# A gated recurrence and a routed expert layer on one core: another order in the sequences, list scatters spread out, another opening

## The reference

```python
def reference(x, ...):                      # x: 8 sequences x 512 tokens x 256, float32
    xn = layernorm(x)
    # recurrence
    g, v, d = xn @ Wg + bg, xn @ Wv + bv, xn @ Wd + bd        # 256 x 256 each
    h = linear_scan(sigmoid(g) * tanh(v), a=0.001 + 0.998 * sigmoid(d))   # along the 512 tokens
    # 8 experts, the best two of each token, and one shared expert
    scores = sigmoid(xn @ gate.T + b + bias)
    top2 -> weights[token, expert]
    y = sum_e weights[:, e] * (gelu(xn @ W1[e].T + b1[e]) @ W2[e].T + b2[e])   # 256 -> 1024 -> 256
    shared = gelu(xn @ Ws1.T + bs1) @ Ws2.T + bs2
    return x + h + y + shared
```

## Time and profile before

| | before |
|---|---|
| median of 3 runs | 729.48 us (728.88 to 731.09) |
| profiled execution | 729.41 us, of which span 727.1 us |
| mean granted TensorE clock | 0.986 |
| busy: TensorE, VectorE, ScalarE, GpSimd | 91%, 72%, 59%, 42% of the span |
| phase 1, opening included | 0 to about 315 us |
| phase 2 | about 315 to 727 us |

### The profile page before, as it was taken

How to read it: one execution, slowest core, us unless ns; L and a number is a source line. 1 busy time by engine, 2 the same in 40 slices (tenths; PEclk the granted TensorE clock), 3 DMA queues, 4 the chain that set the end, 5 groups by cost and what they waited for, 6 DMA issues and landing times.

```text
span 727.1 us, 20160 instructions
## 1 busy us (share of the span) xinstructions
PE 664.5 (91%) x5816; PEld 516.4 (71%) x5817; DVE 523.6 (72%) x1381; ACT 431.7 (59%) x738; POOL 303.5 (42%) x261
## 2 busy tenths in 40 slices
PE   2679898999898999779999999999999999999993
PEld 1246565556555565568888888888888888888773
DVE  4579897979888898866666676666676666666652
ACT  6766767686767766445555555555555555554651
POOL 2015252524343343414464464464464554453521
PEclk9899999999999999999999999999999999999998
DMA  8407170716162624112332332332332332332421
GB/s 266 150 2 188 44 174 32 175 29 173 30 173 36 167 51 123 46 44 50 60 65 53 63 65 52 63 62 54 64 63 53 65 58 58 65 59 52 74 39 22
DMA packets 54172, 57.55 MB, mean 79 GB/s; under 512 B 13204, under 2 KB 48916, under 8 KB 54136
## 3 DMA queue, kind: packets, MB, share of 16 engines
q1 hardware_dynamic: 38456, 38.42, 19.7%
q0 software_dynamic: 15680, 18.69, 16.1%
HBM read 38.53 MB, written 18.55 MB: 79 GB/s over the span
## 4 chain that ended last, share of the span: by engine, by line
PE 60%; DVE 21%; issue 8%; ACT 7%; DMA 1%; DVEq 1%; POOL 0%; ACTq 0%; SPq 0%; POOLq 0%
PE bank L1150 26%; PE bank L1142 24%; DVE W L767 4%; DVE arena L863 3%; PE bank L1169 3%; DVE arena L864 2%; PE bank L1199 2%; ACT W L605 2%; PE bank L1181 2%; ACT arena L569 2%; PE bank L1130 2%; DVE arena L806 1%; DVE small L776 1%; ACT arena L562 1%; DVE arena L795 1%
## 5 line engine op out<-in xcount | busy, mean ns | idle before, releaser
L1150 PE MATMUL bank<-W,arena 128*128 (+1 forms) x2304 | 304.6, 274 | 22.3 <-DVE arena L864 21.7
L1142 PE MATMUL bank<-rows,W 128*128 128x256 f16 (+1 forms) x1920 | 301.3, 295 | 4.6 <-issue 3.3
L1150 PEld LDWEIGHTS bank<-W,arena 128*128 128x128 f16 x2304 | 221.3, 98 | 66.6 <-DVE arena L864 31.7
L1142 PEld LDWEIGHTS bank<-rows,W 128*128 (+1 forms) x1920 | 186.7, 99 | 59.2 <-issue 3.8
L576 ACT ACTIVATE arena<-bank,par 128x256 f32<-128x256 f32 x256 | 133.8, 559 | 83.7 <-PE bank L1142 73.1
L490 POOL DMA_INDIRECT out<-arena,slot_add x64 | 109.5, 1710 | 149.9 <-ACT arena L688 140.2
L863 DVE TENSOR_SCALAR arena<-arena,par 128x256 f16<-128x256 f32 x284 | 101.7, 358 | 83.4 <-ACT arena L576 53.6
L864 DVE SCALAR_TENSOR_TENSOR arena<-arena,par 128x256 f16<-128x256 f32 x284 | 138.8, 489 | 10.1
L432 POOL DMA_INDIRECT lists<-entry,place x64 | 83.5, 1305 | 118.2 <-DVE entry L860 101.1
L475 POOL DMA_INDIRECT rows<-xhl_rows,slot_list x64 | 68.9, 1077 | 46.0 <-DMA slot_list<-lists 22.9
L1130 PE MATMUL bank<-rows,W 128*128 128x512 f16 x288 | 67.1, 392 | 6.2 <-ACT arena L562 6.2
(11 more groups left out here) (158 smaller groups left out, 542.4 us busy)
## 6 DMA issues: line engine op xcount, KB each, us to landing
stage<-in_w SPq DMA_DIRECT2D x32, 512.0 KB, 6.2
b2row<-in_b SPq DMA_DIRECT2D x39, 128.0 KB
arena<-in_x SPq DMA_DIRECT2D x8, 512.0 KB
xhl_rows<-W SPq DMA_DIRECT2D x8, 512.0 KB
out<-arena SPq DMA_DIRECT2D x8, 512.0 KB
W<-in_w SPq DMA_DIRECT2D x4, 512.0 KB, 8.4
lists<-entry,place POOLq DMA_INDIRECT x64
rows<-xhl_rows,slot_list POOLq DMA_INDIRECT x64
```

The costliest lines, as they stand in the source:

```text
L1142: ins = T.matmul(bank_, weights(w, wp * HALF + c * H + j * P, P), rhs[:, 2 * xp + c, :], start=n == 0, stop=n == 3 * KD - 1)
L1150: ins = T.matmul(banks[t // 2][:, (t % 2) * D:(t % 2 + 1) * D], h[:, hp, t * P:(t + 1) * P], weights(w, (2 + wp) * HALF + j * D, D), start ...
```

## The change

`sequence` gets a new order on four engines. In ScalarE's, `squares` of the next set move: one each behind projections 1 and 4 and behind GELUs 0 and 1 (before: behind projections 1, 3, 4 and 5); `normed` and `x_high` move one GELU later, and `score` moves up behind projection 4. In VectorE's, `scan_input(b, ch)` waits for one event less, `places` moves up to stand behind split 0, the `residual`s move from splits 3 and 4 to 2 and 3, the first `low_part` moves from split 5 to 4, and the second stands behind `add_bias`. `scales` shrinks from 13 instructions to 8 (the power of two is taken from the exponent of the sum directly). On TensorE `ranks` moves one projection up, `norm_sum` becomes two accumulating matmuls into bank `ps_l` and also waits for `place_ok`, and the `scan_transposes` and `x_transposes` move one block up each. In the last sequence `places` moves ahead of `shared_result`, the three `tables` parts move from splits 0, 1, 2 to 1, 2, 4, and set 8's preparation moves up.

The eight `scatter`s of a sequence, until now issued back to back, are spread: the first waits for `place_ok`, the others for the event numbers in `SPREAD`, counted from the sequence's start; numbers over 14 lie in the next sequence.

The opening has functions of its own. The two halves of x's transposes go to two banks; 24 and 12 dummy matmuls (`WARM`) are put around them; routing, layer by layer splitting and the recurrence are interleaved. The constant list contents are built in another part of the arena.

```diff
+SMALLEST = float(48 << 23)
+WARM = 24
+SPREAD = {None: (10, 11, 13, 14, 16, 18, 20), SEQS - 2: (9, 10, 11, 12, 13, 14, 15), SEQS - 1: (4, 5, 6, 7, 8, 9, 10)}
-        spare = arena[:, 6144:6656].bitcast(U32)
-        zeros = arena[:, 6656:7168]
+        spare = arena[:, 0:512].bitcast(U32)
+        zeros = arena[:, 512:1024]
+        ps_low16 = ps_e[3][:, :].bitcast(F16)
@@ gpsimd
-            def scatter(b):
+            def scatter(b, c):
                 u = b % 2
-                pool.wait_ge(entry_ok, 2 * b + 2)
-                pool.wait_ge(place_ok, b + 1)
-                for c in range(2 * TPB):
-                    pool.indirect_dma_start(...)
+                if c == 0:
+                    pool.wait_ge(entry_ok, 2 * b + 2)
+                    pool.wait_ge(place_ok, b + 1)
+                else:
+                    pool.wait_ge(ev_act, RING + b * EVENTS + SPREAD.get(b, SPREAD[None])[c - 1])
+                pool.indirect_dma_start(...)
             for b in range(SEQS):
+                for c in range(4, 7):
+                    if b:
+                        scatter(b - 1, c)
                 if b + 1 < SEQS:
                     rstd(b + 1)
-                scatter(b)
+                if b:
+                    scatter(b - 1, 7)
                 if b + 1 < SEQS:
                     fill_entries(b + 1)
+                for c in range(4 if b + 1 < SEQS else 8):
+                    scatter(b, c)
@@ scalar
+            def opening():
+                for i in range(2):
+                    projection(0, 0, i)
+                for part in range(2):
+                    high_part(0, 0, part)
+                projection(0, 0, 2)
+                decay(0, 0)
+                projection(0, 0, 3)
+                projection(0, 0, 4)
+                high_part(0, 1, 0)
+                projection(0, 0, 5)
+                high_part(0, 1, 1)
+                act.wait_ge(spare_out, 64)
+                gelu_wide(0, 0, 0)
+                decay(0, 1)
+                score(0)
+                squares(1, 0, 0)
+                gelu_wide(0, 0, 1)
+                squares(1, 0, 1)
+                gelu_wide(0, 0, 2)
+                normed(1, 1)
+                gelu_wide(0, 0, 3)
+                squares(1, 1, 0)
+                gelu_wide(0, 0, 4)
+                squares(1, 1, 1)
+                act.wait_ge(xhl_out, 16)
+                x_high(1)
+                ...
             def sequence(b, u, last_=False):
                 for i in range(PROJ):
                     projection(b, u, i)
                     if i in (2, 5):
                         decay(b, i // 3)
-                    if not last_:
-                        if i == 1:
-                            squares(b + 1, 0, 0)
-                        if i >= 3:
-                            squares(b + 1, (i - 2) // 2, (i - 2) % 2)
+                    if i == 1:
+                        squares(b + 1, 0, 0)
+                    if i == 4:
+                        score(b)
+                        squares(b + 1, 0, 1)
                 for i in range(KH):
                     gelu_wide(b, u, i)
-                    if i == 0:
+                    if i in ((1, 2) if last_ else (0, 1)):
+                        squares(b + 1, 1, i - last_)
+                    if i == 1 and not last_:
                         normed(b + 1, 1 - u)
-                    if i == 1:
+                    if i == 2 and not last_:
                         act.wait_ge(xhl_out, b * 16 + 16)
                         x_high(b + 1)
-                    if 3 <= i < 7:
-                        high_part(b + 1, (i - 3) // 2, (i - 3) % 2)
+                    k = i - 4 if last_ else i - 3
+                    if 0 <= k < 4:
+                        high_part(b + 1, k // 2, k % 2)
@@ vector
+            def opening():
+                for part in range(5):
+                    best_two(0, part)
+                scales(0)
+                variances(1, 1)
+                for part in range(2):
+                    low_part(0, 0, part)
+                scan_input(0, 0)
+                scan(0, 0)
+                for part in range(2):
+                    low_part(0, 1, part)
+                scan_input(0, 1)
+                split_wide(0, 0)
+                scan(0, 1)
+                split_wide(0, 1)
+                places(0, 0)
+                split_wide(0, 2)
+                dve.wait_ge(bs2_in, 16)
+                add_bias(0, 0)
+                own.settle()
+                residual(0, 0, 0)
+                split_wide(0, 3)
+                residual(0, 0, 1)
+                split_wide(0, 4)
+                scales(1)
+                x_low(1)
+                split_wide(0, 5)
+                low_part(1, 0, 0)
+                split_wide(0, 6)
+                low_part(1, 0, 1)
+                split_wide(0, 7)
+                add_bias(1, 1)
             def sequence(b, u, last_=False):
                 if last_:
                     for part in range(5):
                         best_two(b, part)
+                for part in range(2):
+                    low_part(b, 1, part)
+                if last_:
+                    places(b, u)
+                shared_result(b - 1, 0)
+                shared_result(b - 1, 1)
                 ...
                 for i in range(KH):
                     split_wide(b, i)
                     if i == 0:
+                        if not last_:
+                            places(b, u)
                         scan(b, 1)
+                    if i == 1 and not last_:
+                        scales(b + 1)
+                    if i == 3 and last_:
+                        scales(b + 1)
                     if i == 2:
-                        places(b, u)
-                        x_low(b + 1)
+                        if not last_:
+                            x_low(b + 1)
+                        dve.wait_ge(o_out, b * 16)
+                    if i in (2, 3):
+                        residual(b, u, i - 2)
+                    if last_ and i in (1, 2, 4):
+                        tables((1, 2, 4).index(i))
+                    if i == 4 and not last_:
+                        low_part(b + 1, 0, 0)
+                    if last_ and i >= 5:
+                        low_part(b + 1, (i - 5) // 2, (i - 5) % 2)
                 if last_:
                     keep_entries(0, 0, first=True)
                     parameters(0, 0)
+                    low_part(b + 1, 1, 1)
                 else:
                     add_bias(b + 1, 1 - u)
+                    low_part(b + 1, 0, 1)
@@ tensor
-                    if i == 0 and not last_:
-                        pe.wait_ge(xT_ok, b * 2 + 2)
-                        norm_sum(b + 1, ps_t)
+                    if i == (4 if first else 2 if last_ else 0):
+                        pe.wait_ge(place_ok, b + 1)
+                        norm_sum(b + 1, ps_l[:, 128:130])
+                    if i == 1:
+                        pe.wait_ge(scan_ok, b * 2 + 2)
+                        scan_transposes(b, 0)
                     if i == 2:
-                        pe.wait_ge(scan_ok, b * 2 + 2)
-                        ...
-                    if i == 3:
                         pe.wait_ge(r_ok, b * 2 + 1)
                         scan_transposes(b, 1)
-                    if i == 5 and not last_:
+                    if i == 4 + first and not last_:
                         ...
                         x_transposes(b + 1, 0)
-                    if i == 6 and not last_:
+                    if i == 5 + first and not last_:
                         ...
                         x_transposes(b + 1, 1)
...
+            for i in range(WARM):
+                T.matmul(ps_e[2][:, 0:P], ones[:, :], ones[:, :], start=True, stop=True)
+            pe.wait_ge(xhi_ok, 1)
+            x_transposes(0, 0)
             pe.wait_ge(xhl_ok, 1)
-            x_transposes(0, 0)
-            pe.wait_ge(xT_ok, 1)
-            x_transposes(0, 1)
+            x_transposes(0, 1, ps_low16)
+            for i in range(WARM // 2):
+                T.matmul(ps_e[2][:, 0:P], ones[:, :], ones[:, :], start=True, stop=True)
```

144 lines of the change are left out of this document (52 added, 92 removed).

## The result

The changed kernel takes 710.78 us (median; 710.6 to 710.98), against 730.29 for the kernel before beside it: a ratio of 0.9716, 95% interval 0.9683 to 0.9749. The forecast was 715 with 706 to 723.

The account below looks back on a forecast made before the run. Phase 2 was taken as TensorE-bound, phase 1 as TensorE and VectorE waiting in turn: 729.4 - 7.7 (opening) - 8.5 (middle sequences) + 1.9 (last sequence) = 715.1. Forecast 715 us, own range 710 to 720, overall 706 to 723.

Parts of the forecast that it names:

- the sum: Whole kernel: 729.4 less 7.7 for the opening and 8.5 for middle sequences, plus 1.9 for the last sequence, makes 715.1.
- (c): Middle sequences: `scales` falls from 2.73 to 1.3 us, VectorE reaches split 2 before TensorE asks, the 0.97 wait goes.
- (d): Middle sequences: TensorE then runs from its own work, ten groups and three transposes; split 7 at 19.2 instead of 20.8.
- (b): Middle sequences: `norm_sum` behind `layer2(0)` waits for later squares, a stall of 0.2, plus 0.3 for two matmuls.
- the prediction's sentences on the Trainium skill: TensorE's clock: activity releases throttling; dummies cut 5.51 to 3.9, new pauses cost 1 to 3; 714 to 717.
- the upper end: Last sequence: phase 2 starts 45.3 after split 7, or 46 with a slow group.
- TensorE didn't become the bound: Rival, middle sequences: VectorE's junction has unseen slack, period falls to TensorE's 31.7, time 705; chance 0.11.
- The period didn't stay: Rival, middle sequences: stalls at `norm_sum` and residual take the gains of (a) and (c), time 722; chance 0.20.
- The slower rival: Rival: scatters beside VectorE's junction hold VectorE, adding 3.6 to 4.8 us a period, time 740; chance 0.07.

Follow-up runs that it names:

- the long `scales` run: Changed kernel with five more instructions in each `scales` chain of the middle sequences, as long as before: 718.29 us, ratio 0.9851 to the kernel before.
- three edits of a line or two each: Changed kernel with sequence 0's norm sum one block earlier, tables' third part ahead of `scales`, last sequence's `score` behind projection 2, all at once: 704.71 us.
- the two kernels with spread scatters: On the last chip: the changed kernel once more, 711.36 us, and the changed kernel with norm sum, tables and `score` edits together, 704.71 us.
- the norm sum, tables and `score` runs: Changed kernel with one edit each: sequence 0's norm sum one block earlier, 708.77 us; tables' third part ahead of `scales`, 709.07; last sequence's `score` behind projection 2, 709.99.

## Why the prediction held, point by point

The time came out 4.2 us below the forecast, near the lower end of the forecast's own range of 710 to 720. By the marks the change brought 18.3 of span where the sum had 14.3: 2.0 more in the opening, 0.2 more in the middle, 0.8 less lost in the last sequence, and 0.9 in phase 2, which the sum put at nothing.

**The middle sequences: the sum was right, the shares were not.** The period is 33.6 as forecast, the first `layer2` at 3.75 (forecast 3.8), split 7 at 19.33 (19.2), VectorE's stretch behind it 14.33 (14.35). Over the whole stretch 8.68 came where I had 8.5. But the four periods now on hand say where it is from (those without a wait of the kind above):

| | `scales` of 13 | `scales` of 8 |
|---|---|---|
| ScalarE's new order, the other engines as before | 33.8 | 33.0 |
| the changed kernel's order on all engines | 34.6 | 33.6 |

From 35.1 ScalarE's order takes 1.3 and the short chain 0.8 to 1.0; the rest of the new order, taken together, costs 0.6 to 0.8. The rows above point at `places` and at the transposes moved forward for this cost; neither was run alone. In (c) I let `places` in front of split 1 go at nothing, and in (d) I counted a third group of transposes ahead of `layer2(5)` without noting that the kernel before has only two there. My sum held the transposes as a duration and 0.7 for the norm sum, where (b) makes only 0.5 and the rows show 0.47 without a stall (171.07 to 171.54), so it came out near, in part by luck; I didn't see that this part was a loss, and would have called it neutral.

**(c), the slack of the chain.** I let VectorE reach split 2 at 9.7 and TensorE ask for it at 10.2. Measured are 9.9 and 10.2, and the 0.3 between them is no slack of the chain: residual 0 stands behind it too, and the long `scales` run passed its 1.05 on in full.

**The opening: right places, 2.0 too little.** Each mark came somewhat early: projections at 15.43 (16), the first scan at 27.02 (28.0), the first `layer2` at 32.17 (33.3), the wait ahead of `layer2(5)` 3.65 (3.9), sequence 1's scan at 65.39 (66.9, and I had taken 0.5 off for the clock). The opening is the term of the sum that was most mis-sized, 7.7 against 9.75, and it is its front: the norm sum of set 0 stands at 18.88, in the middle of the projections, and `scales(0)` is through at 20.76 where I had 21.7.

**The clock there.** By the prediction's sentences on the Trainium skill the dummies would bring up to 1.6 and the new pauses cost 1 to 3, for a time of 714 to 717. Measured: the dummies 1.0; the pause of 3.65 costs its two groups 1.3 in one execution and 2.2 in another (2.20 and 2.05, 2.74 and 2.38, against 1.47), of which sequence 1 shows 0.8 as the difference. The time lies below 714 all the same, since the rest of the sum came out larger.

**The last sequence.** The tables end 33.1 after split 7 (33), TensorE waits 4.09 for the rows (3.7), phase 2 starts at 45.2 (45.3 to 46). I took the upper end for a slow first group; its first 24 matmuls took 3.49 in all, less than before (4.22), which is most of the 0.9 that phase 2 gained. The 1.31 that `places` waits for `score` was not in my walk: I moved `places` on VectorE and didn't ask when ScalarE does `score`.

**The rivals.** TensorE didn't become the bound: six of its waits, 5.7 us in all, remain between 68 and 270 us (fourteen and 16.0 before). The 31.7 of that rival was too low besides: with 1.1 of waiting in a period of 33.6, TensorE's own work fills 32.5. Its 705 also lay outside my range of 706 to 723. The period didn't stay. The slower rival had its mechanism wrong, VectorE's splits being 750 ns beside and without scatters. Its direction, that it matters where the scatters run, was right, and it is the opposite of what I feared: together they are what hurts on one chip, and spread no run shows them to hurt. My forecast put the spreading at nothing, and on the chips of the first runs it is worth 0 to 1.5 us, on another one 22. That this term stayed out of the result is luck of the chip: on the last one the kernel before and the changed one are 23.0 us apart and not 19.5, and no profile of the kernel before there tells how much of that belongs to the scatters.

## What to carry to other kernels

Ask of a moved step what stands behind it on its own engine as well as who waits for it: the same move can be a gain by the one and a loss by the other, and a sum that comes out right doesn't say that each part was worth making. A new wait in a hand-written order is often cured by one place: three edits of a line or two each, read from the three waits of the profile after, brought another 6.7 us. And a kernel whose executions agree on one chip is to be run on a second before a part of it is called harmless.

## What the runs showed of the hardware

On one chip, waits of VectorE and ScalarE for signals of TensorE that had long been due ended only when GpSimd was through with eight indirect DMAs that it issued back to back: 1.4 to 1.6 us after the last of them in all five cases of the one profile, 1.4, 1.1 and 0.8 after it in the three of the other. The engines stood idle for 4.2 to 6.5 us each, and the signals had been due for 2.9 to 5.0. Only the kernels that issue the eight together had them: 12 executions of 12 in one (729.81 to 736.04, where the undisturbed time is 712.3), by their times four of six in another (713.55 to 724.24); the two kernels with spread scatters had none in twelve executions (704.3 to 705.51 and 710.75 to 711.74). The kernel before spreads there by as much as such a wait or two (729.27 to 736.07), but also on the chip of the norm sum, tables and `score` runs (730.07 to 734.16), and its one profile is from the first occasion and has no such wait. No profile from the other chips shows a wait of this kind, though three kernels with the eight together were run there. The rows say that TensorE's signals come late, to two engines at once, while one of VectorE's reached TensorE at once; why, and why only behind some rows of scatters, is open. So is whether it belongs to the chip: the record has it on one occasion only, and nothing tells the two apart.

The second thing is smaller: after one and the same pause of 3.65 us TensorE's clock came back earlier in one execution than in another (granted 0.75 from 50 to 56 us, against 0.64), and the rest of the kernel stands 0.8 us later in the second. A difference of that size between two kernels, each read in one profile, isn't evidence.
